# Logits from x2 less its mean, a norm_b row through DRAM, slot statistics in the loop, spectral sums on POOL

## The reference

```python
x = x + cross_attention(layernorm(x), ctx)       # 128 rows x 256; 12544 context rows
x = x + long_convolution(layernorm(x))           # x2 is the sum here
x = x + soft_moe(layernorm(x))

# long_convolution, ORDER = 2
p = h @ proj_w + proj_b                          # 128 x 768: v, p1, p2
for stage in 0, 1:
    v = irfft(rfft(v) * rfft(filter[stage])) * p[stage + 1]

# soft_moe, 16 experts x 64 slots = 1024 slots
z  = (x2 - mean) * rstd
xn = z * norm_g + norm_b
se = ((slot_embeds - mean) * rstd * slot_g + slot_b) * scale
logits   = xn @ se.T                             # 128 x 1024
dispatch = softmax(logits, over the rows);  combine = softmax(logits, over the slots)
slots = dispatch.T @ xn
eout  = (gelu(slots @ Wg + bg) * (slots @ Wu + bu)) @ Wd + bd
out   = combine @ eout
```

## Time and profile before

| | |
|---|---|
| median of 3 runs | 193.52 us (193.42 to 193.71) |
| the profiled execution | 192.96 us, its span 190.9 us |
| TensorE busy | 185.7 us, 97% |
| VectorE busy | 125.7 us, 66% |
| ScalarE busy | 108.9 us, 57% |
| POOL busy | 82.4 us, 43% |
| TensorE clock granted | 1.00 in all slices |
| HBM read | 46.73 MB, 245 GB/s over the span |

### The profile page before, as it was taken

How to read it: one execution, slowest core, us unless ns; L and a number is a source line. 1 busy time by engine, 2 the same in 40 slices (tenths; PEclk the granted TensorE clock), 3 DMA queues, 4 the chain that set the end, 5 groups by cost and what they waited for, 6 DMA issues and landing times.

```text
span 190.9 us, 3968 instructions
## 1 busy us (share of the span) xinstructions
PE 185.7 (97%) x1268; PEld 145.5 (76%) x1268; DVE 125.7 (66%) x272; ACT 108.9 (57%) x226; POOL 82.4 (43%) x61
## 2 busy tenths in 40 slices
PE   6999999999999999999999999999999999999994
PEld 4888999999999999999999989974544555454463
DVE  3567988797777778777777888743673513515542
ACT  3568687677777767767776443967358521112210
POOL 2787978688777678877768012100000000000000
PEclk9999999999999999999999999999999999999999
DMA  5999957737784873984493399999999999993300
GB/s 185 321 347 367 357 177 277 256 129 232 246 276 142 281 248 116 353 236 150 135 240 91 124 352 385 353 374 367 382 365 383 280 353 289 273 208 99 75 0 27
DMA packets 25051, 47.01 MB, mean 246 GB/s; under 512 B 1616, under 2 KB 12112, under 8 KB 25040
## 3 DMA queue, kind: packets, MB, share of 16 engines
q1 hardware_dynamic: 23808, 43.52, 68.7%
q10 hardware_dynamic: 1232, 3.35, 7.2%
HBM read 46.73 MB, written 0.13 MB: 245 GB/s over the span
## 4 chain that ended last, share of the span: by engine, by line
PE 93%; ACT 2%; DMA 2%; DVE 1%; issue 0%; SPq 0%; ACTq 0%
PE bank L662 15%; PE bank L413 11%; PE bank L676 6%; PE bank L454 6%; PE bank L458 6%; PE bank L456 6%; PE bank L426 6%; PE bank L430 6%; PE bank L428 6%; PE bank L439 6%; PE bank L724 2%; PE bank L714 2%; PE bank L549 2%; DMA W_sb<-in_L_xattn_W_dram 2%; PE bank L568 2%; ACT seT L881 1%
## 5 line engine op out<-in xcount | busy, mean ns | idle before, releaser
L998 POOL TENSOR_TENSOR c_lo<-raw,c_hi 128x1024 fp32r<-128x1024 f32 (+1 forms) x25 | 54.0, 2160 | 20.1 <-ACT c_hi L793 20.1
L1076 DVE TENSOR_TENSOR cT_lo<-bank,cT_hi 128x512 fp32r<-128x512 f32 (+1 forms) x50 | 31.7, 675 | 10.6 <-ACT cT_hi L820 9.5
L820 ACT ACTIVATE cT_hi<-bank 128x512 fp32r<-128x512 f32 (+1 forms) x48 | 25.7, 584 | 10.1 <-PE bank L413 10.1
L454 PE MATMUL bank<-c_hi,pT_hi 128*128 128x258 f32 x98 | 29.9, 305 | 0.0
L458 PE MATMUL bank<-c_hi,pT_lo 128*128 128x258 f32 x98 | 27.7, 282 | 0.0
L456 PE MATMUL bank<-c_lo,pT_hi 128*128 128x256 f32 x98 | 27.5, 281 | 0.0
L993 POOL TENSOR_TENSOR c_hi<-raw,zero 128x512 fp32r<-128x512 f32 (+1 forms) x25 | 25.7, 1027 | 1.4 <-DMA raw<-in_ctx_dram 1.4
L413 PE MATMUL bank<-tab,raw 128*128 128x128 f32 x196 | 25.8, 273 | 0.2 <-DVE cT_lo L1076 0.2
L827 ACT ACTIVATE pT_hi<-bank 128x512 fp32r<-128x512 f32 (+1 forms) x25 | 14.7, 590 | 14.2 <-PE bank L439 14.1
L413 PEld LDWEIGHTS bank<-tab,raw 128*128 128x128 f32 x196 | 22.1, 141 | 0.9 <-issue 0.3
L426 PE MATMUL bank<-cT_hi,q_hi 128*128 128x512 f32 (+1 forms) x50 | 21.5, 430 | 0.0
(11 more groups left out here) (178 smaller groups left out, 289.7 us busy)
## 6 DMA issues: line engine op xcount, KB each, us to landing
raw<-in_ctx_dram SPq DMA_DIRECT2D x24, 512.0 KB, 3.8
bias<-biases_dram ACTq DMA_DIRECT2D x10, 320.0 KB, 7.5
late_gu<-in_L_ffn_Wg_dram SPq DMA_DIRECT2D x3, 1024.0 KB, 10.7
late_gu<-in_L_ffn_Wu_dram SPq DMA_DIRECT2D x3, 1024.0 KB, 11.2
late_d<-in_L_ffn_Wd_dram SPq DMA_DIRECT2D x3, 1024.0 KB, 13.6
early_gu<-in_L_ffn_Wg_dram SPq DMA_DIRECT2D x4, 512.0 KB, 4.9
early_gu<-in_L_ffn_Wu_dram SPq DMA_DIRECT2D x4, 512.0 KB, 4.6
early_d<-in_L_ffn_Wd_dram SPq DMA_DIRECT2D x4, 512.0 KB, 4.9
```

What stands on the lines that cost most here:

```text
L454: nc.tensor.matmul(bank[6 + r][:, 0:D + 2], ph, c_hi[:, slot, t, :], start=(t == 0), stop=False)
L820: nc.scalar.activation(cT_hi[:, g % 2, h, 0:n], bank[h][:, 0:n], ACT.Copy).then_inc(cThi_rdy, 1)
L998: nc.gpsimd.tensor_tensor(c_lo[:, slot, 0:nt, :], raw[:, slot, 0:nt, :], c_hi[:, slot, 0:nt, 0:D].bitcast(fp32), ALU.subtract).then_inc(cl ...
L1076: nc.vector.tensor_tensor(cT_lo[:, g % 2, h, 0:n], bank[h][:, 0:n], cT_hi[:, g % 2, h, 0:n].bitcast(fp32), ALU.subtract).then_inc(cTlo_rdy, 1)
```

## The change

- **Logits.** TensorE transposes x2 less its mean, without rstd and norm_g (norm_g is multiplied into the column scales of seT). Logits leave PSUM through `finish_logits`: bank times rstd plus a row `beta`, which VectorE adds from `comb`. That row holds norm_b's share: for each slot (sum of b_row * se minus mean * sum of b_row) * rstd of the slot, with b_row = norm_b * slot_g * scale. The product of norm_b with slot_b is the same for every slot and cancels in both softmaxes.
- **The row beta.** `b_col` is computed at the start, stored to DRAM by ScalarE's queue and loaded as a broadcast row `b_row`. VectorE's `slot_dot` in the loop multiplies it with each tile of se. `beta` (128 x 8) is stored to `rows_dram` with 4-byte runs and loaded into `comb` as a broadcast over 128 partitions.
- **Piece 0** goes the way of the others: logits, transpose, maximum, exponential, transpose, copy. `transposed_logits`, `first_logits`, `shift_logits`, `dispatch_sums`, `first_logits_back`, `ones_sq` and `diag` go. Half of a part of `logits(2)` moves ahead of `gather(0)`.
- **Slot statistics** all stand in the loop (two `bn_stats` and two `slot_dot` a round); `slot_variance` and `row_sum` follow the loop, `slot_shift` the last step. The tiles of se are normalised in two halves and transposed between other work.
- **Spectral products** are added by POOL, so each half needs two inverse matmuls. p2 is made by ScalarE and POOL, x1 by ScalarE.

```diff
@@ TensorE
-            keep_busy(1)
             transpose_xh(pe, 1)
+            transpose_slots(0)
             pe.wait_ge(ld_pw, 32)
...
+                if o == 0:
+                    pe.wait_ge(seT_rdy, 1)
                     project(2 * D, 3 * D, 7)
+                    pe.wait_ge(spec_rdy, 2 * ORDER)
+                else:
+                    transpose_slots(1)
+                    transpose_slots(2)
                 for h in range(2):
+                    pe.wait_ge(sum_rdy, 2 * o + h + 1)
                     for i, inv in enumerate((inv_s, inv_c)):
-                        pe.wait_ge(prod_rdy, 4 * o + 2 * h + i + 1)
-                        for j in range(2):
-                            last = nc.tensor.matmul(bank[CONV_BANK[h]][:, 0:P], inv, prod[:, h, i, j, :],
-                                                    start=(i == 0 and j == 0), stop=(i == 1 and j == 1))
+                        last = nc.tensor.matmul(bank[CONV_BANK[h]][:, 0:P], inv, prod[:, h, i, 0, :],
+                                                start=(i == 0), stop=(i == 1))
...
+            for k in range(DK):
+                pe.wait_ge(xc_rdy[k], 1)
+                nc.tensor.transpose(bank[XC_BANK[k]][:, 0:P], x_sb[:, cols(k)], ident).then_inc(xcT_ps, 1)
...
-            transposed_logits()
-            first_logits()
+            pe.wait_ge(seT_rdy, 2)
+            for k in range(DK):
+                pe.wait_ge(xcT_rdy[k], 1)
+                logits(0, (k,))
             logits(1, (0,))
-            shift_logits()
+            transpose_logits(0)
             logits(1, (1,))
+            transpose_dispatch(0)
+            pe.wait_ge(seT_rdy, 4)
+            logits(2, (0,), 0)
             gather(0)
-            dispatch_sums()
             transpose_logits(1)
...
-                    logits(2)
-                    first_logits_back()
+                    logits(2, (1,), 0)
+                    logits(2, range(DK), 1)
@@ ScalarE
             rows_hi(None, 0, 0, GT)
+            act.wait_ge(bcol_rdy, 1)
+            act.dma_start(rows_dram[SLOTS:SLOTS + D].rearrange("(k p) -> p k", p=P), b_col[:, :],
+                          allow_slow_non_contiguous=True).then_inc(st_brow, 16)
...
+            act.wait_ge(st_brow, 16)
+            act.dma_start(b_row, rows_dram[SLOTS:SLOTS + D].rearrange("(a n) -> a n", a=1).broadcast_to([P, D])
+                          ).then_inc(ld_brow, 16)
...
+            normalise((0, 1))
+            act.wait_ge(beta_rdy, 1)
+            act.dma_start(rows_dram[0:SLOTS].rearrange("(j p) -> p j", p=P), beta[:, :],
+                          allow_slow_non_contiguous=True).then_inc(st_beta, 16)
+            normalise((2, 3))
             for k in range(DK):
                 act.wait_ge(xhT_ps, k + 2)
                 nc.scalar.activation(xhT[:, k, :], bank[XH_BANK[1][k]][:, 0:P], ACT.Copy).then_inc(xhT_rdy, 1)
+            spectrum(0)
             spectrum(1)
...
+            slots_evacuated(0)
+
+            act.wait_ge(st_beta, 16)
+            act.dma_start(comb[:, :], rows_dram[0:SLOTS].rearrange("(a n) -> a n", a=1).broadcast_to([P, SLOTS])
+                          ).then_inc(ld_beta, 16)
+            act.wait_ge(rstd_rdy, 3)
+            act.wait_ge(proj_ps, 4)
+            nc.scalar.activation(p_sb[:, 2 * D:3 * D], bank[7][:, 0:D], ACT.Identity, scale=rstd[:, 0:1]
+                                 ).then_inc(p2s_rdy, 1)
+            normalise((4, 5, 6, 7))
+            act.wait_ge(linv_rdy, 1)
+            nc.scalar.activation(x1[:, :], xn[:, :], ACT.Identity, scale=linv[:, 0:1]).then_inc(x1_rdy, 1)
+            for n in range(1, 4):
+                slots_evacuated(n)
@@ POOL
+            def spectral_sum(o, h):
+                pool.wait_ge(prod_rdy, 4 * o + 2 * h + 2)
+                nc.gpsimd.tensor_tensor(prod[:, h, :, 0, :], prod[:, h, :, 0, :], prod[:, h, :, 1, :], ALU.add
+                                        ).then_inc(sum_rdy, 1)
@@ VectorE
             norm(0, x_sb[:, :], xh[:, :], xh_rdy)
+            def slot_columns():
+                dve.wait_ge(ld_scale, 16)
+                link(nc.vector.tensor_scalar(col[:, 1:3, :], col[:, 1:3, :], scale_b[:, 0:1], None, ALU.mult))
+                nc.vector.tensor_tensor(b_col[:, :], col[:, 1, :], col[:, 4, :], ALU.mult).then_inc(bcol_rdy, 1)
+                dve.wait_ge(bcol_rdy, 1)
+                for i in (1, 2):
+                    last = nc.vector.tensor_tensor(col[:, i, :], col[:, i, :], col[:, 3, :], ALU.mult)
+                last.then_inc(gs_rdy, 1)
...
                 for u in range(RING):
                     step(n, FIRST + u)
-                    if u == 0:
-                        slot_stats(n, 0)
+                    if u < 2:
+                        slot_stats(n, 3 * u)
+                    else:
+                        slot_dot(n, 3 * (u - 2))
+            slot_variance()
+            row_sum()
             for i in range(FIRST + RING * LOOPS, GROUPS + 2):
                 step(None, i)
...
+            slot_shift()
             update_output(None, LAST - 1)
...
+            nc.vector.tensor_scalar(x_sb[:, cols(0)], x2[:, cols(0)], mv[:, 0:1], None, ALU.subtract
+                                    ).then_inc(xc_rdy[0], 1)
+            dve.wait_ge(xcT_ps, 1)
+            nc.vector.tensor_copy(xnT[:, 0, :], bank[XC_BANK[0]][:, 0:P]).then_inc(xcT_rdy[0], 1)
...
+            def finish_logits(n):
+                lo, hi = PIECES[n]
+                dve.wait_ge(L_ps, n + 1)
+                dve.wait_ge(ld_beta, 16)
+                nc.vector.scalar_tensor_tensor(out=comb[:, lo * P:hi * P], in0=bank[L_BANK[n]][:, 0:(hi - lo) * P],
+                                               scalar=rstd[:, 0:1], in1=comb[:, lo * P:hi * P],
+                                               op0=ALU.mult, op1=ALU.add).then_inc(L_rdy, 1)
```

More of the change, by code:

```diff
@@ L502, in _, with transpose_slots @@
                 spectrum(o)
-            keep_busy(1)
             transpose_xh(pe, 1)
+            def transpose_slots(n):
+                k, half = SE_PIECE[n]
+                pe.wait_ge(se_rdy, 4 * (half + 1))
+                if n == 3:
+                    pe.wait_ge(seT_rdy, 2)
+                for j in range(4):
+                    last = nc.tensor.transpose(bank[SE_BANK[n]][:, j * P:(j + 1) * P],
+                                               se[:, 4 * half + j, k * P:(k + 1) * P], ident)
+                last.then_inc(seT_ps, 1)
+            transpose_slots(0)
             pe.wait_ge(ld_pw, 32)
@@ L551, in _ @@
                     last.then_inc(conv_ps, 1)
-            for n in range(4):
-                transpose_slots(n)
-            keep_busy(6)
-            pe.wait_ge(z_rdy, 1)
+            transpose_slots(3)
+            keep_busy(4, 4)
             for k in range(DK):
-                last = nc.tensor.transpose(bank[(7, 1)[k]][:, k * P:(k + 1) * P], xh[:, k * P:(k + 1) * P], ident)
-            last.then_inc(zT_ps, 1)
-            keep_busy(4)
-            pe.wait_ge(xnT_rdy, DK)
-            pe.wait_ge(seT_rdy, 4)
@@ L571, in logits @@
                     last.then_inc(L_ps, 1)
-            def transposed_logits():
-                for k in range(DK):
-                    last = nc.tensor.matmul(bank[LT_BANK[0]][:, 0:P], seT[:, k, 0:P], xnT[:, k, :],
-                                            start=(k == 0), stop=(k == DK - 1))
-                last.then_inc(LT_ps, 1)
-            def first_logits():
-                for k in range(DK):
-                    nc.tensor.matmul(bank[3][:, 0:P], xnT[:, k, :], seT[:, k, 0:P], start=(k == 0), stop=False)
@@ L1135, in _ @@
                 step(None, i)
-            dve.wait_ge(ld_scale, 16)
-            for i in (1, 2):
-                last = nc.vector.tensor_scalar(col[:, i, :], col[:, i, :], scale_b[:, 0:1], None, ALU.mult)
-            last.then_inc(gs_rdy, 1)
             dve.wait_ge(ld_se, 16)
@@ L1270, in _ @@
                     if p == 0:
+                        finish_logits(2)
                         dispatch_lo(1)
```

209 lines of the change are left out of this document (103 added, 106 removed).

## The result

The changed kernel takes 210.95 us (median of 4, 210.24 to 212.3) against 193.47 for the one before beside it: ratio 1.0892, 95% interval 1.0834 to 1.0949. The forecast was 196.8 and a range of 192.0 to 200.0: the side is right, the size is not. Of 17.5 us more, 3.3 were foreseen. (Medians here are over all runs; ratios and intervals leave disturbed runs out.)

What follows compares the result with a forecast made beforehand. TensorE, with 93% of the chain, was taken to bound the kernel, so other engines count only where it waits. Engines -0.4 plus beta's transfers +3.7 gave +3.3 on the 193.52 median: 196.8 us, range 192.0 to 200.0.

Steps and rivals of the forecast that it cites:

- The start, +0.35: Before the W² products: VectorE's slot columns, held by POOL's c_hi, delay them; +0.7 if held, 0 if not, middle taken.
- The store of b_col and the load of b_row ... 0.: At the start, on ScalarE's queue: both fall where ScalarE has idle time, so they cost 0.
- The loop, 0: Attention loop: one more bn_stats and two dots per round of four steps, delay covered by TensorE's lead; 0.
- The last steps, +1.2: Loop end to step 23: added VectorE statistics, held by POOL's c_lo, delay the probabilities; +1.2 us, +0.4 without any hold.
- Convolutions, 0: Spectral products: half the product pieces go, but POOL's sum stands between; 0, bounds -0.5 to +0.5 us.
- Variance to gate, -1.35: Variance to first gate product: seT conversions spread ahead, rstd by POOL off the path; -1.35 us, bounds -0.8 and -1.9.
- Pair 0, -0.6: Pair 0: a quarter of logits(2) moves into a wait, the back-transpose goes; -0.6 us, bounds -0.1 and -0.7.
- The two transfers of beta, +3.7: Beta's store and broadcast load on ScalarE's queue: row there at 129.6, wanted at 125.9; +3.7 us, bounds 0 and +7.2.
- that is 9.5 us: Beta's store, issue to landing: 112.0 to 121.5, its packets one for one with the weights'; 3.4 over the 6.1 available.
- The rival of grouped packets: Beta's store packets served together, store 5.3 us, transfers in time and costing 0; faster, 193.1 us; chance 0.32.
- The clock after the wait: Sign of being wrong: TensorE's clock below 1.00 after the long wait, which nowhere showed before; priced at nothing.
- the forecast gain of the engines alone: Sum of all terms without beta's two transfers: 0.35 + 1.2 + 0 - 1.35 - 0.6 = -0.4 us.

Runs made afterwards that it cites:

- the columns late: Against the kernel without either store, the slots' five small column operations run after the steps ahead of the loop; 195.32 us, ratio 1.0021 to the kernel before.
- the kernel with rows by products: Whole change, but TensorE makes b_row and beta's row by products with the identity, not through DRAM; 199.63 us, ratio 1.0301 to the kernel before.

## Why the prediction was wrong, step by step

- **What bounds the kernel.** Right in the main: the large excesses showed as TensorE waiting; the smaller ones also as work of its own in a worse place and as its clock.
- **The start, +0.35.** Mechanism half right (held by POOL's c_hi, 0.94 us for the first operation). The third pair of operations was priced at a part of "some 0.5" and can meet c_lo: +2.5 to 5 us with the clock. In the changed kernel's own profile it did not: what is late there are the products of W squared themselves.
- **"The store of b_col and the load of b_row ... 0."** Wrong: 3.3 us in the changed kernel's profile, 4.8 by the ratios. I asked only whether ScalarE is idle there, not how long 272 packets take or what they do to the reads beside them. The store lands after 13.4 us, and from 14 to 22 us the DMA engines move a third of the bytes.
- **The loop, 0.** Right: with the columns late, four steps take 16.58 us (4.52, 4.17, 3.76, 4.13 between maxima), before 16.57.
- **The last steps, +1.2.** 0.7, inside the bounds, and by the mechanism: the drawn-out TENSOR_SCALAR is there (109.28 to 110.12, c_lo ends at 110.09), TensorE waits 0.51 us for the probabilities, and with these operations one step later both are gone.
- **Convolutions, 0.** +0.8, outside the bound of 0.5, 0.7 of it in the second order: the slots' transposes moved ahead of the last products had no price at all in my sum.
- **Variance to gate, -1.35.** -0.73 without the stores, just less than the lower bound of -0.8.
- **Pair 0, -0.6.** -0.6.
- **The two transfers of beta, +3.7: the step that failed.** Its course was as written: the store late, ScalarE idle, p2 and four normalisations behind it, finish_logits released by the comb load. Its size was 10.9 to 11.4. The term mis-sized is "that is 9.5 us": 17.9 measured, and even the upper bound of 13 was under it. The course of the packets was right at first: the store goes out at 116.28, its first packets come 4 us later (3.9 forecast), and then one for one. What was wrong is the 0.08 and 0.047 us for each of the weights' packets beside it: they hold for full traffic, and this store takes the traffic away. Spread out, the same store took 10.9, near the forecast, and cost 3.4 us; my slip of 3.5 for 9.5 us, and 1.4 more, gives 4.9, so the room before the wait hurts was also larger than the 6.1 and 0.35 us that I gave it. That neighbouring four-byte writes hold up the traffic was not in any row of before, whose only stores are the two of the result. The rival of grouped packets could not have given the lower bound as I wrote it: a turn of the store's group would stand behind a group of the weights'.
- **The clock after the wait, "which I price at nothing".** It fell, as the list of signs of being wrong had it. In the changed kernel's profile four slot transposes and the eight inverse products behind the wait take 1.12 and 1.91 us; the same take 0.60 and 1.30 before it, at 1.00. That makes 1.1 us, an estimate from these four rows, inside the 11.2.
- **Luck.** None helped: the forecast gain of the engines alone (-0.4) was not there either, +0.2 in the profile without stores and +1.6 by the ratio.

## What to carry to other kernels

Look at a small store by its runs in DRAM, not by its bytes: beside 4 KB in 1,024 neighbouring pieces of four bytes, a core's weight stream fell from 197 packets in a microsecond to 154 in six (125 to 131 us), and the same 4 KB as eight rows after one transpose cost nothing that could be measured. A resource that a trace doesn't show in use (a strided store beside a full queue) deserves a bound as wide as the wait behind it can grow. And when work is moved into a gap, price it by what the gap was hiding: transposes, products and a copy moved that way cost 0.7 to 2 us each here.

## What the runs showed that I had not expected

- Writes of four bytes side by side: 1,024 landed after 17.9 and 17.9 us (19.2 where nobody waits), 256 after 13.4 and 12.4. 64 bytes apart 10.9; in pieces of 32 bytes 5.9; as a read 11.3.
- While they drain, reads of another queue on the same engines fall to 7 packets a microsecond, at 80% of the engines' time. Behind b_col's store the reads are held down for eight microseconds after its last packet was taken (101 GB/s and not 303).
- A VectorE operation on 128x2 numbers took 2.10 us under POOL's 2.19, and the gap of 2.42 us that it made on TensorE was followed by a granted clock of 0.50 from 12 to 16 us and later; a wait of 1.96 us in the kernel with rows by products likewise (0.61 on average from 20 to 24 us).
- The first four products of W squared take 1.14 to 2.08 us in kernels with the same start, at a granted clock shown as 1.00. Most of the spread of all kernels here, 192.9 to 196.1 for the one before, may come from there; that was not tested.
